# Row squares of two layer norms on ScalarE, centred output weights, constant matmuls ahead of the keys, and new orders on every engine

## The reference

```python
q = proj(layernorm(x), Wq, bq); k = proj(ctx, Wk, bk); v = proj(ctx, Wv, bv)
scores = clip(q @ k.T / sqrt(32), -50, 50)          # masked entries: -50
probs = softmax(scores)
delta = rs * ((probs @ v) @ Wo.T + bo)              # rs = clip(residual_scale, 0, 0.3)
delta = (delta - mean(delta)) / sqrt(var(delta) + 1e-5) * gamma + beta
x1 = x + delta
h = layernorm(x1)
gate = softmax(h @ router.T) * (its two largest)
out = x1 + sum_e gate_e * (silu(h @ down_e.T) @ up_e)
```

## Time and profile before

| | before |
|---|---|
| median of 3 runs | 213.22 us (212.46 to 214.08) |
| the profiled execution's own time | 212.69 us |
| its span, first to last instruction | 210.7 us |
| PE busy | 193.4 us (92%) |
| DVE busy | 162.2 us (77%) |
| ACT busy | 90.8 us (43%) |
| POOL busy | 114.0 us (54%) |
| DMA moved | 19.40 MB, mean 92 GB/s |

### The profile page before, as it was taken

How to read it: one execution, slowest core, us unless ns; L and a number is a source line. 1 busy time by engine, 2 the same in 40 slices (tenths; PEclk the granted TensorE clock), 3 DMA queues, 4 the chain that set the end, 5 groups by cost and what they waited for, 6 DMA issues and landing times.

```text
span 210.7 us, 3718 instructions
## 1 busy us (share of the span) xinstructions
PE 193.4 (92%) x1316; PEld 143.1 (68%) x1316; DVE 162.2 (77%) x339; ACT 90.8 (43%) x164; POOL 114.0 (54%) x166
## 2 busy tenths in 40 slices
PE   7599979999889999999899999999998799989693
PEld 8478858545476886776588875667764678867671
DVE  1899464764776988948976789489888899899994
ACT  2384256851487412287642016383105332345340
POOL 5732199394759719437601335094235963598550
PEclk9859999999999999999999999999999999999769
DMA  5999700035640231000042100004030010122207
GB/s 213 360 334 350 277 18 0 12 104 178 177 160 0 105 89 33 0 3 0 0 115 72 42 3 0 0 16 134 19 111 1 36 67 0 53 101 100 100 37 264
DMA packets 12006, 19.40 MB, mean 92 GB/s; under 512 B 2258, under 2 KB 4306, under 8 KB 11988
## 3 DMA queue, kind: packets, MB, share of 16 engines
q1 hardware_dynamic: 11988, 19.17, 27.0%
HBM read 14.45 MB, written 4.72 MB: 91 GB/s over the span
## 4 chain that ended last, share of the span: by engine, by line
PE 72%; DVE 18%; DMA 3%; ACT 3%; issue 3%; SPq 0%; DVEq 0%
PE ps_r L384 53%; PE ps_t L408 5%; PE ps_v L481 4%; PE ps_r L454 4%; DMA stage<-ctx_t 3%; PE ps_v L468 3%; DVE xs L1025 3%; ACT stage L720 2%; DVE n_st L1028 2%; DVE x1t_lo L955 1%; PE ps_v L522 1%; DVE hidt_lo L955 1%; DVE rz L998 1%; DVE compare L1053 1%; DVE gate L1067 1%
## 5 line engine op out<-in xcount | busy, mean ns | idle before, releaser
L384 PE MATMUL ps_r<-hst_hi,wq_hi 128*128 128x512 f32 x64 | 26.4, 413 | 2.6 <-ACT stage L720 2.6
L1324 POOL TENSOR_TENSOR xs<-xs,beta_bc 128x512 f32<-128x512 f32 x16 | 22.0, 1398 | 11.5 <-issue 8.7
L1328 POOL TENSOR_TENSOR attt_lo<-wk,attt_hi 128x512 fp32r<-128x512 f32 x16 | 21.3, 1357 | 12.6 <-ACT attt_hi L729 12.6
L708 ACT ACTIVATE q_sb<-ps_r,bq_sb 128x512 f32<-128x512 f32 x16 | 11.0, 686 | 33.5 <-PE ps_r L384 33.5
L384 PE MATMUL ps_r<-wo_lo,attt_hi 128*128 128x512 f32 x64 | 25.3, 395 | 0.0
L384 PE MATMUL ps_r<-hst_hi,wq_lo 128*128 128x512 f32 x64 | 25.3, 395 | 0.0
L384 PE MATMUL ps_r<-wo_hi,attt_lo 128*128 128x512 f32 x64 | 25.3, 395 | 0.0
L384 PE MATMUL ps_r<-hst_lo,wq_hi 128*128 128x512 f32 x64 | 25.2, 394 | 0.0
L384 PE MATMUL ps_r<-wo_hi,attt_hi 128*128 128x512 f32 x64 | 25.2, 394 | 0.0
L522 PE MATMUL ps_v<-dr_hl,x1t_hi 128*128 128x272 f32 x64 | 18.6, 354 | 1.9 <-DVE rz L998 1.0
L1353 POOL TENSOR_TENSOR xs<-up_out,xs 128x512 f32<-128x512 f32 x12 | 16.9, 1420 | 5.7 <-ACT up_out L758 5.7
(11 more groups left out here) (117 smaller groups left out, 458.8 us busy)
## 6 DMA issues: line engine op xcount, KB each, us to landing
wk<-rz_scratch SPq DMA_DIRECT2D x32, 128.0 KB, 2.7
out<-xs SPq DMA_DIRECT2D x16, 256.0 KB, 2.0
xs<-x SPq DMA_DIRECT2D x3, 1024.0 KB, 5.6
xs<-x SPq DMA_DIRECT2D x2, 512.0 KB, 4.0
wk<-wk_t SPq DMA_DIRECT2D x1, 1024.0 KB, 8.3
stage<-wq_t SPq DMA_DIRECT2D x1, 1024.0 KB, 10.5
xs<-wv_t SPq DMA_DIRECT2D x1, 1024.0 KB, 10.2
xs<-wo_t SPq DMA_DIRECT2D x1, 1024.0 KB, 10.8
```

The source lines that it names most:

```text
L384: last = pe.matmul(dst, w, m, start=start and i == 0, stop=stop and i == n - 1)
L708: act.activation(q_sb[:, m, :], ps_r[ring_r.bank(f"Q{b}{m}")][:, :], ACT.Identity, bias=bq_sb[:, m:m + 1]).then_inc(q_ok, 1)
L1324: pool.tensor_tensor(xt, xt, beta_bc[:, :], ALU.add).then_inc(xb_ok, 1)
L1328: pool.tensor_tensor(attt_lo[:, :, c, :], att[:, c, :].rearrange("p (t n) -> p t n", t=NT), attt_hi[:, :, c, :].bitcast(F32), ALU.subtract ...
```

## The change

- Front: 22 constant matmuls in place of 14, and 5 more between the first eight transposes and `keys(0)`: 27 in all.
- The columns of the output weights are centred once: `centre_wo(c)` subtracts from each row of the transposed weight its mean (DVE, three instructions for each of four chunks), and bo is centred in the same way. A projected row then has the mean zero, so its variance needs only the sum of squares. `centre(b, t)` goes; in its place ACT squares the bank with the sum as a second output (`projected_squares`), and DVE multiplies by gamma in one instruction (`scaled`).
- The sum of an x1 row comes as a second output of the instruction that makes x1 (`accum_out=n_sum`), and ACT computes the sum of (sum - 512 * x1)^2 (`x1_squares`), which is 512^3 times the variance. The bn_stats and bn_aggr of x1 go from DVE.
- The square's full result is not used; it goes to `cen`, which is the buffer `hs`. So `hs_norm` of batch 3 waits for the squares of batch 0, where it waited for x1.
- All four low parts of the query weights are made by DVE. bo comes by one DMA to 33 partitions in place of two to one partition each.
- The calls on PE, ACT, DVE, POOL and SP and the three rings stand in another order.

```diff
-WARM = 14
+WARM = 22
+WARM_MORE = 5
...
+            for _ in range(WARM_MORE):
+                pe.matmul(ps_r[3][:, 0:P], average[:, :], average[:, :], start=True, stop=True)
...
 RING_R = (
-    "K0 K1 K2 K3 Q00 Q01 S00 S01 S02 S03 Q02 Q03 S04 S05 S06 S07 V0 V1 Q10 Q11 S10 S11 S12 S13 Q12 Q13 "
-    "S14 S15 S16 S17 W00 W01 W02 W03 Q20 Q21 S20 S21 S22 S23 Q22 Q23 S24 S25 S26 S27 W10 W11 W12 W13 Q30 "
-    "Q31 S30 S31 S32 S33 Q32 Q33 S34 S35 S36 S37 U00 W20 W21 W22 W23 U01 U02 W30 W31 U03 W32 U10 U11 U12 "
-    "U13 W33 U20 U21 U22 U23 U30 U31 U32 U33")
+    "K0 K1 K2 K3 Q00 Q01 V0 V1 Q02 Q03 S00 S01 S02 S03 S04 S05 S06 S07 Q10 Q11 S10 S11 S12 S13 Q12 Q13 "
+    "S14 S15 S16 S17 W00 W01 W02 W03 Q20 Q21 Q22 Q23 S20 S21 S22 S23 S24 S25 S26 S27 W10 W11 W12 W13 Q30 "
+    "Q31 S30 S31 S32 S33 Q32 Q33 S34 S35 S36 S37 W20 W21 W22 W23 U00 U01 U02 U03 U10 U11 W30 W31 W32 W33 "
+    "U12 U13 U20 U21 U22 U23 U30 U31 U32 U33")
...
-            sp.dma_start(bo_raw[0:1, :], rows(bo, 1)).then_inc(rs_bo_in, 16)
-            sp.dma_start(bo_raw[32:33, :], rows(bo, 1)).then_inc(rs_bo_in, 16)
+            sp.dma_start(bo_raw[:, :], rows(bo, 33)).then_inc(rs_bo_in, 16)
...
+            def projected_squares(b, t):
+
+
+                n = NT * b + t + 1
+                act.wait_ge(mm_full, ring_r.count(f"W{b}{t}", every=True))
+                if b:
+                    act.wait_ge(d_ve_ok, n - NT)
+                    act.wait_ge(n_sq_ok, n - NT)
+                act.activation(cen[:, t, :], ps_r[ring_r.bank(f"W{b}{t}")][:, :], ACT.Square,
+                               accum_out=d_sq[:, t:t + 1]).then_inc(d_sq_ok, 1)
+
+            def x1_squares(b, t):
+
+
+                n = NT * b + t + 1
+                act.wait_ge(x1_ok, n)
+                if b:
+                    act.wait_ge(n_ve_ok, n - NT)
+                act.activation(cen[:, t, :], xs[:, bass.ds(NT * b + t, 1), :], ACT.Square, bias=n_sum[:, t:t + 1],
+                               scale=-float(H), accum_out=n_sq[:, t:t + 1]).then_inc(n_sq_ok, 1)
...
-                act.wait_ge(wo_in, 16)
+                act.wait_ge(wo_mid_ok, c + 1)
...
-            def centre(b, t):
+            def scaled(b, t):
 
                 n, bank = NT * b + t + 1, ps_r[ring_r.bank(f"W{b}{t}")]
                 if (b, t) == (0, 0):
                     dve.wait_ge(rs_step, 4)
-                hold(mm_full, ring_r.count(f"W{b}{t}", every=True))
-                dve.bn_stats(d_st[:, t, :], bank[:, :]).then_inc(d_st_ok, 1)
-                hold(d_st_ok, n)
-                dve.bn_aggr(d_mv[:, t, :], d_st[:, t, :]).then_inc(d_mv_ok, 1)
-                dve.wait_ge(d_mv_ok, n)
-                dve.scalar_tensor_tensor(cen[:, t, :], bank[:, :], d_mv[:, t, 0:1], gamma_rs[:, :],
-                                         ALU.subtract, ALU.mult).then_inc(mm_free, 1)
+                dve.wait_ge(d_sq_ok, n)
+                dve.tensor_tensor(cen[:, t, :], bank[:, :], gamma_rs[:, :], ALU.mult).then_inc(mm_free, 1)
 
             def residual(b, t):
 
...
                 dve.wait_ge(xb_ok, n)
                 dve.wait_ge(mm_free, ring_r.count(f"W{b}{t}"))
                 dve.wait_ge(d_rstd_ok, n)
-                dve.scalar_tensor_tensor(x_tile, cen[:, t, :], d_rstd[:, t:t + 1], x_tile, ALU.mult, ALU.add
-                                         ).then_inc(x1_ok, 1)
-                hold(x1_ok, n)
-                dve.bn_stats(n_st[:, t, :], x_tile).then_inc(n_st_ok, 1)
-                hold(n_st_ok, n)
-                dve.bn_aggr(n_mv[:, t, :], n_st[:, t, :]).then_inc(n_mv_ok, 1)
+                dve.scalar_tensor_tensor(x_tile, cen[:, t, :], d_rstd[:, t:t + 1], x_tile, ALU.mult, ALU.add,
+                                         accum_out=n_sum[:, t:t + 1]).then_inc(x1_ok, 1)
...
+            def centre_wo(c):
+
+                if c == 0:
+                    dve.wait_ge(wo_in, 16)
+                dve.bn_stats(w_st[:, c, :], wo_raw[:, c, :]).then_inc(w_st_ok, 1)
+                hold(w_st_ok, c + 1)
+                dve.bn_aggr(w_mv[:, c, :], w_st[:, c, :]).then_inc(w_mv_ok, 1)
+                dve.wait_ge(w_mv_ok, c + 1)
+                dve.tensor_scalar(wo_raw[:, c, :], wo_raw[:, c, :], w_mv[:, c, 0:1], None, ALU.subtract
+                                  ).then_inc(wo_mid_ok, 1)
...
-            for c in range(2, KC):
+            for c in range(KC):
...
-            dve.tensor_scalar(rs_sq[:, :], rs_sb[:, :], rs_sb[:, :], None, ALU.mult).then_inc(rs_step, 1)
+            dve.tensor_scalar(rs_sq[:, :], rs_sb[:, :], rs_sb[:, :], 1.0 / H, ALU.mult, ALU.mult).then_inc(rs_step, 1)
+            dve.bn_stats(w_st[0:33, KC, :], bo_raw[:, :]).then_inc(bo_mid_ok, 1)
+            dve.wait_ge(bo_mid_ok, 1)
+            dve.bn_aggr(w_mv[0:33, KC, :], w_st[0:33, KC, :]).then_inc(bo_mid_ok, 1)
+            dve.wait_ge(bo_mid_ok, 2)
+            dve.tensor_scalar(bo_raw[:, :], bo_raw[:, :], w_mv[0:33, KC, 0:1], None, ALU.subtract
+                              ).then_inc(bo_mid_ok, 1)
...
-                pool.tensor_scalar(d_ve[:, t:t + 1], d_mv[:, t, 1:2], rs_sq[:, :], EPS, ALU.mult, ALU.add
+                if (b, t) == (0, 0):
+                    pool.wait_ge(rs_step, 3)
+                pool.wait_ge(d_sq_ok, n)
+                pool.tensor_scalar(d_ve[:, t:t + 1], d_sq[:, t:t + 1], rs_sq[:, :], EPS, ALU.mult, ALU.add
...
-                pool.tensor_scalar(n_ve[:, t:t + 1], n_mv[:, t, 1:2], 1.0, EPS, ALU.mult, ALU.add
+                pool.wait_ge(n_sq_ok, n)
+                pool.tensor_scalar(n_ve[:, t:t + 1], n_sq[:, t:t + 1], 1.0 / float(H) ** 3, EPS, ALU.mult, ALU.add
...
-            for c in range(2):
-                pool.wait_ge(wq_hi_ok, c + 1)
-                pool.tensor_tensor(wq_lo[:, c, :], wq_raw[:, c, :], wq_hi[:, c, :].bitcast(F32), ALU.subtract
-                                   ).then_inc(wq_lo_ok, 1)
```

527 lines of the change are left out of this document (281 added, 246 removed).

## The result

| | before | after |
|---|---|---|
| median | 213.44 us (4 runs, 212.46 to 214.08) | 207.34 us (4 runs, 205.65 to 208.60) |
| ratio to before | | 0.9722 (0.9667 to 0.9778) |
| profiled execution: time, span | 212.69, 210.7 us | 206.56, 204.6 us |
| mean granted clock over the span | 0.968 | 0.980 |
| busy PE, DVE, ACT, POOL | 193.4, 162.2, 90.8, 114.0 us | 190.7, 143.4, 111.8, 109.1 us |

The change makes the kernel 2.8% faster. The forecast was 203.8 us with a range from 199.5 to 209.5: the direction is right and the time lies in the range, but it is 3.5 us above the forecast: of the 9.4 us that were forecast, 6.1 came.

A forecast was written before the change was run, and what follows sets the result against it. PE, busy 193.4 of 210.7 us, was taken as the bound. Front 2.3, middle 1.5, end waits 2.5 and end clock 3.1 sum to 9.4 us: span 201.3, time 203.8, range 199.5 to 209.5.

The forecast's parts named there:

- Front: Start of kernel: added matmuls keep the clock, keys(0) takes 3.6 us, first query at 19.0, 2.3 us earlier.
- The doubt about the six low parts: Before the first query: DVE's six low parts, if stretched to 0.9 us each, give 20.3 and a gain of 1.0.
- DVE and ACT: Whole kernel: DVE busy time falls by about 21 us, to 141; ACT's rises from 91 to 115 us.
- the upper bound: x1's second output on DVE: at most one more instruction of 0.18 us, 3 us in all; 0.1 was taken.
- Middle: From 67.5 to 142.7 us: PE's idle 2.1 us falls to 0.6, 1.5 won; the 2.6 up to 67.5 stay.
- End: After 142.7 us: 3.0 of PE's 5.5 us idle stay, 2.5 won; the clock's fall goes too, 3.1 us.
- The price of the half clock at the end: After 193.7 us: 6.53 us busy at half the clock, about half of it, 3.1 us, taken as won whole.
- rivals 1 and 2: 1: reordering gives nothing, waits move to ACT, 209.4, chance 0.14; 2: clock falls in front anyway, 206.3, chance 0.12.
- Rival 3: ACT waits in a round trip for x1, 1.7 us on 10 of 16 tiles: slower, about 221, chance 0.06.
- Chances: Forecast (201 to 206) 0.60, rival 1 (207 to 210) 0.14, rival 2 0.12, slower 0.06, no change 0.08.
- the prediction's own signs: Profile after: keys(0) 3.6 us, first query 19.0, squares 0.75, DVE near 140, ACT near 115, plus the two end signs.

## Why the prediction was right, and where its steps were off

- **Front: right.** Forecast 2.3 us and 19.0 for the first query; it came at 18.68, 2.6 us earlier. DVE's second cleaning instruction took 0.75 us and ended at 14.97, and keys(1) could start at 15.29. That POOL's low parts had to go for this was not so: with the front alone they stayed, and the instruction took 0.74 us. There it had begun at 13.85, ahead of POOL's 14.34; in the kernel before it began at 14.16, behind POOL's 14.10, and took 1.80. What the move of the low parts gave is seen at the first query, 19.26 with the front alone and 18.68 after. The doubt about the six low parts did not come true: four took 2.48 us together. That the gain reaches the end was assumed without a word. In the kernel after it does, 3.0 us; in the kernel before no gain of the front alone is clear of the noise.
- **DVE and ACT: right in the sum.** DVE is at 143.4 us (forecast 141), of which 4.7 us are the five stretched steps (138.7 with the additions held); the sum had also left out the 1.6 us that the prediction itself gave the second outputs; ACT at 111.8 (115). A square is 0.60 us from the bank and 0.72 from x1, each with a second instruction of 0.2 us behind it that reads the sum; the two overlap (150.32 + 0.60 with 150.81). On DVE the second output costs a read of 0.08 us. The Trainium skill (VectorE: DVE Perf Modes, "Two Vector instructions with no wait between them") says of such an op that it is two instructions, and the trace shows both; it costs half of the 0.18 us that I had put as the upper bound.
- **Middle: right in size, not in place.** Forecast 1.5 us from 67.5 to 142.7; it is 1.9 (2.1 to 0.2). But up to 67.5 PE stands 3.6 us, not 2.6: exp costs 1.20, 1.21 and 0.64 us at three places. I had written of "two or three places, for about 1 us each" and then left the sum at 2.6.
- **End: the step that failed.** "3.0 of 5.5 us stay, 2.5 us won" and "the fall of the clock should go as well, 3.1 us". PE's idle time is 5.5 us as before, so none of the 2.5 us came. The clock falls at 196.5; PE is busy 3.61 us at half of it in place of 6.53, so counted as the prediction counts (half of the busy time) about 1.5 of the 3.1 us came. The step reasoned from DVE's busy share (90% to 70%), and that share did fall. But the last gates do not wait for a free DVE: their chain is as long as its own steps, and these were stretched by POOL, which the new order lets reach its additions of batch 2 just then. I had kept 2.1 us for the gated units as untouched; they became 3.6, and after the one of 2.8 the clock fell again. With POOL held back these waits are gone and the mean clock is 0.992 to 0.994 in all four executions, which gave 2.5 us of the 3.5 missing. A stretched step was there to be read in the kernel before as well: its last gating instruction took 1.40 us, beside two additions, and the mean over eight hides it. There it cost little, as PE was busy until the units were ready.
- **The price of the half clock at the end: too high.** I took half of 6.53 us. In the kernel before PE's passes at half clock ran beside the gating and ended at 204.37 us, just as the units were ready (204.32); with the front alone, at full clock, PE stood 1.43 and 2.34 us there instead. The half clock is not free for all that: where no step is stretched the units are ready at 201.37 and 201.38 us in the two runs with the additions held, and PE begins on them at 202.42 at half clock and at 201.44 at full clock, 1.0 us apart. It also costs where PE's passes are the last link, as the last six up passes of the kernel after, 0.43 us apart in place of 0.23, 1.2 us.
- **Rivals.** The times of rivals 1 and 2, 209.4 and 206.3, bracket the result, but neither mechanism is it: the clock held in front, and in the middle PE's waits for DVE went and did not turn into waits for ACT's squares or high parts. Rival 3, ACT's round trip, shows in none of PE's longer waits. That the change could make the kernel slower was not absurd: in the old orders its norms cost 1.5 to 2.8%.
- **Chances: the range held, the forecast did not.** 207.34 lies outside the 201 to 206 that had 0.60, in the 207 to 210 given to rival 1 with 0.14, whose mechanism it is not. That the range holds it is owed to the room made for rivals. By the prediction's own signs (PE waits near 3 us, no stretch at 0.5 at the end) the end was wrong.

## What to carry to other kernels

A busy share says how much work an engine has, not how long its chain is. For the last stage, list the chain's steps with their durations in the very place, and compare each with what the same instruction takes elsewhere; where one takes several times as long, look at what the other engines do in the same microseconds, here POOL, and hold that neighbour back, a change of two lines. Then ask whether the step is what the next engine waits for: in the kernel after it was, in the kernel before PE was busy until the step was done. Orders and engine loads are tuned as a pair: the new orders without the new norms, and the norms without the orders, each made the kernel slower. And one profile shows one launch: take the clock of all executions before you say that a front keeps or loses it.
